# Neighbourhood attention: row maxima of single heads in two score banks, and a ring of five banks for the turned products

## The reference, cut to what matters

```python
x = x + _L0_conv_ref(_gn(x), ...)      # 12 heads over all 1024 tokens
x = x + _L1_conv_ref(_gn(x), ...)      # the layer of the change
x = x + _L2_conv_ref(_gn(x), ...)
x = x + _L3_conv_ref(_gn(x), ...)

# _L1_conv_ref
k_cat = jnp.concatenate([k, reg_k], axis=-2)
v_cat = jnp.concatenate([v, reg_v], axis=-2)
mask = make_neighbourhood_mask(KERNEL, KERNEL, h, w)          # 7 x 7, clipped at the edges
scores = jnp.einsum('bnqe,bnke->bnqk', q, k_cat) * scale
scores = jnp.where(mask_cat[None, None], scores, NEG_INF)
attn = jax.nn.softmax(scores, axis=-1)
o = jnp.einsum('bnqk,bnke->bnqe', attn, v_cat)
o = o.transpose(0, 2, 1, 3).reshape(n, h, w, nh * e)
return o @ out_w.T + out_b
```

## Time and profile before

| | us |
|---|---|
| median of three timed runs | 8417.23 |
| the three runs | 8416.32, 8417.23, 8431.45 |
| the profiled execution | 8455.42 |
| its span | 8453.7 |
| the stretch of `attend_win` in it | 2713 to about 3487 |

### The profile page before, as it was taken

How to read it: one execution, slowest core, us unless ns; L and a number is a source line. 1 busy time by engine, 2 the same in 40 slices (tenths; PEclk the granted TensorE clock), 3 DMA queues, 4 the chain that set the end, 5 groups by cost and what they waited for, 6 DMA issues and landing times. The chain is left out here.

```text
span 8453.7 us, 163553 instructions
## 1 busy us (share of the span) xinstructions
PE 7140.6 (84%) x56704; PEld 4354.6 (52%) x56704; DVE 4964.6 (59%) x7151; ACT 3849.1 (46%) x7081; POOL 2019.5 (24%) x2406
## 2 busy tenths in 40 slices
PE   3999999999866999479989999997686799999998
PEld 2555555555444656245555555553332455555555
DVE  3655555555444666545555555553878566666665
ACT  1444444444511555324444444443011577777776
POOL 3344334344210000043443443431111000000000
PEclk7999999999977898769899999998666899999999
DMA  7666766766457655567667667663122545455453
GB/s 176 127 131 115 132 131 123 138 118 123 76 166 188 123 115 112 128 132 137 123 123 130 125 121 138 120 126 78 74 77 68 128 118 129 114 124 124 114 129 83
DMA packets 502140, 1026.32 MB, mean 121 GB/s; under 512 B 80616, under 2 KB 276905, under 8 KB 460793
## 3 DMA queue, kind: packets, MB, share of 16 engines
q1 hardware_dynamic: 454198, 932.07, 50.4%
q0 software_dynamic: 47360, 86.53, 6.3%
HBM read 658.36 MB, written 358.93 MB: 120 GB/s over the span
## 5 line engine op out<-in xcount | busy, mean ns | idle before, releaser
L1616 DVE TENSOR_REDUCE a_nmp<-a_S 128x2 f32<-128x1024 f32 x1536 | 1878.4, 1224 | 1294.9 <-PE a_S L1461 1279.0
L1717 ACT ACTIVATE a_PROB<-a_T 128x512 f32<-128x512 f32 x3072 | 1667.8, 595 | 1918.7 <-PE a_T L1440 1778.4
L1310 POOL CAST a_RF<-a_RL 32x512 fp32r<-32x512 f32 x1536 | 1294.9, 843 | 1097.2 <-DVE a_RL L1644 1005.1
L2486 DVE CUSTOM_DVE_ANT_0 a_X<-a_S,a_mask 128x1024 f32<-128x1024 f32 x768 | 909.9, 1222 | 569.7 <-PE a_S L2382 566.2
L1436 PE MATMUL a_T<-a_QW,a_KW 64*128 64x512 f32 x3072 | 810.0, 519 | 283.5 <-ACT a_PROB L1717 206.4
L2527 ACT ACTIVATE a_PROB<-a_T 128x512 f32<-128x512 f32 x1536 | 836.2, 602 | 386.0 <-PE a_T L2396 386.0
L1436 PEld LDWEIGHTS a_T<-a_QW,a_KW 64*128 64x128 f32 x3072 | 313.4, 192 | 1292.2 <-issue 1289.2
L1474 PE MATMUL a_O<-a_PROB,a_V 128*32 128x512 f32 x6144 | 916.9, 672 | 2.5 <-ACT a_PROB L1717 2.5
L2396 PE MATMUL a_T<-a_ident,a_X 128*128 128x128 f32 x6144 | 824.3, 277 | 102.3 <-DVE a_OSB L2503 98.3
L2396 PEld LDWEIGHTS a_T<-a_ident,a_X 128*128 128x128 f32 x6144 | 670.9, 141 | 303.8 <-issue 285.5
L1461 PEld LDWEIGHTS a_S<-a_KV,a_QV 64*128 64x128 f32 x6144 | 660.1, 202 | 123.9
(11 more groups left out here) (179 smaller groups left out, 9120.8 us busy)
## 6 DMA issues: line engine op xcount, KB each, us to landing
a_QV<-a_part_rows SPq DMA_DIRECT2D x384, 256.0 KB, 7.6
a_rel_rows<-a_RF SPq DMA_DIRECT2D x96, 1024.0 KB, 9.3
a_K<-part_rows SPq DMA_DIRECT2D x576, 128.0 KB, 3.8
a_part_rows<-a_part SPq DMA_DIRECT2D x48, 1024.0 KB, 10.9
a_QV<-a_part_rows SPq DMA_DIRECT2D x384, 128.0 KB, 8.1
a_QV<-a_rel_rows SPq DMA_DIRECT2D x384, 128.0 KB, 7.0
a_QW<-a_rel_rows SPq DMA_DIRECT2D x192, 256.0 KB, 9.3
a_mask<-L_mask SPq DMA_DIRECT2D x48, 1024.0 KB, 10.5
```

Of the source, the lines that this page charges most:

```text
L1310: nc.gpsimd.tensor_copy(dst, src).then_inc(permuted, 1)
L1616: nc.vector.tensor_reduce(nmp[:, qh, c, 2 * pr:2 * pr + 2, kh], S[:, pr], AX.X, ALU.max).then_inc(s_done, 1)
L1717: nc.scalar.activation(PROB[:, s % PRING, 2 * pr + sd], T[:, slot(("st", s, pr, sd))], ACT.Exp).then_inc(t_act, 1)
L2486: nc.vector.tensor_tensor_reduce(out=X[:, v % 2, c, g], in0=S[:, sd].rearrange("p a b -> p (a b)"), in1=mask[:, n % 2, g, c], scale=1.0, s ...
```

## The change

The straight products go from pairs to single heads. A turn has MAXIMA = 2 * G = 8 of them, each one matmul of 256 or 284 columns into one bank, and S has two banks instead of four; single n waits for the reduction of single n - 2. DVE reduces each head by itself (one maximum, 128 x 226 or 128 x 284). ITEMS gives singles 0 to 3 to kc = 0, 4 and 5 to kc = 1, 6 and 7 to kc = 2, which are the same heads at the same steps. The two banks go to the ring: RING = 5, so a tile in T waits for the tile five places back in SEQ. The order of SEQ, the tails and all other work stay. From L786 on, line numbers are smaller by one in the changed kernel.

```diff
-    RING, PRING, BUFS = 3, 3, 3
+    RING, PRING, BUFS = 5, 3, 3
...
-    ITEMS = {0: (0, 1), 1: (2,), 2: (3,)}
+    MAXIMA = 2 * G
+    ITEMS = {0: (0, 1, 2, 3), 1: (4, 5), 2: (6, 7)}
...
-        S = ctx.enter_context(nc.psum_tensor(f"{name}_S", [P, 2, 2, BANK], F32))
+        S = ctx.enter_context(nc.psum_tensor(f"{name}_S", [P, 2, BANK], F32))
...
             def straight(t, i):
                 u, quad = divmod(t, QUADS)
-                tile, pr = divmod(i, 2)
-                n, s = 4 * t + i, u % BUFS
+                tile, g = divmod(i, G)
+                n, s = MAXIMA * t + i, u % BUFS
...
                 need(pe, s_done, n - 1)
                 alone(pe)
                 at, width, _, _ = SPANS[(quad // 2, tile)]
-                for sd in range(2):
-                    g = 2 * pr + sd
-                    last = nc.tensor.matmul(S[:, n % 2, sd, 0:width],
-                                            Q_[0:ROWS, s, g, WIDE * quad + P * tile:WIDE * quad + P * tile + P],
-                                            K[0:ROWS, s, g, NEAR * quad + at:NEAR * quad + at + width], start=True, stop=True)
-                last.then_inc(s_ready, 1)
+                nc.tensor.matmul(S[:, n % 2, 0:width],
+                                 Q_[0:ROWS, s, g, WIDE * quad + P * tile:WIDE * quad + P * tile + P],
+                                 K[0:ROWS, s, g, NEAR * quad + at:NEAR * quad + at + width], start=True, stop=True
+                                 ).then_inc(s_ready, 1)
...
             def row_max(t, i):
-                tile, pr = divmod(i, 2)
-                n = 4 * t + i
+                tile, g = divmod(i, G)
+                n = MAXIMA * t + i
                 _, _, at, width = SPANS[(t % QUADS // 2, tile)]
                 eng.wait_ge(s_ready, n + 1)
-                nc.vector.tensor_reduce(nm[:, t % 2, tile, 2 * pr:2 * pr + 2], S[:, n % 2, :, at:at + width], AX.X, ALU.max,
+                nc.vector.tensor_reduce(nm[:, t % 2, tile, g:g + 1], S[:, n % 2, at:at + width], AX.X, ALU.max,
                                         negate=True).then_inc(s_done, 1)
 
             def combine(t):
                 e = t % 2
-                eng.wait_ge(s_done, 4 * t + 4)
+                eng.wait_ge(s_done, MAXIMA * (t + 1))
```

More of the change, by code:

```diff
@@ L854, in _ @@
             pe.wait_ge(wide_set, 1)
-            for i in range(4):
+            for i in range(MAXIMA):
                 straight(0, i)
             turn_max(0)
-            for i in range(4):
+            for i in range(MAXIMA):
                 straight(1, i)
```

## The result

| | before | after |
|---|---|---|
| median of five timed runs, us | 8417.2 | 8512.2 |
| range of the five | 8397.8 to 8449.5 | 8494.0 to 8521.7 |
| ratio | | 1.0089 (95% interval 1.0071 to 1.0108) |
| the profiled execution | 8455.4 | 8494.0 |
| the stage in it (first score product to the end of the last projection) | 772.5 | 830.5 |

The change makes the kernel slower by 75 us (60 to 91), which is the ratio's 0.89% of 8417. The two medians themselves are 95 us apart; in the later experiments the kernel before had medians of 8433.6 (19 runs), 8434.7 (24) and 8436.1 (13), so the 8417.2 of the table is some 18 us low. The forecast was 8467, with 8432 to 8525 as its range. The stage, which is all that the change touches, is 58 us longer in the two profiled executions.

What follows compares the result with a forecast made beforehand. The prediction took the stage to be bound by a chain through three engines, none of them full. Four quad terms gave 2.07 us a unit, x 24 units = +50 us on 8417, so 8467 us, range 8432 to 8525.

Steps and rivals of the forecast that it cites:

- the mechanism: Step 0: third and fourth singles wait for the first two reductions; V comes 1.04 or 1.18 us after r0.
- projection, then 226: Quad with a projection, then 226 columns: V at 3031.26 for 3031.00, +0.26 us.
- projection, then 284: Quad with a projection, then 284 columns: 0.14 us more after r0, 0.05 more before, +0.35 us.
- sums: Quad behind the sums: r0 moves 0.63 us earlier; +0.18 or +0.56 us by unit, middle +0.37 taken.
- reciprocals: Quad behind the turned reciprocals: DVE multiplies outputs first, r0 at 3023.44, V at 3024.48 for 3023.39, +1.09 us.
- unit: One unit of the neighbourhood stage: its four quads add 2.07 us, 32.5 us for 30.4.
- rival 2: TensorE's pauses keep the clock low through the reciprocals' quad: some 1.5 us a unit, 8503; chance 15%, 3% for worse.
- The ring: Five banks remove the tail tiles' wait for the casts: 2 x 0.58 + 0.63 + 0.39 = 2.18 us a unit.
- L785's waits: Score matmuls wait for reductions some 0.4 us each, near 100 us for 2.1; forecast wrong if under 40.
- waits of the tails: The tail tiles' 50.2 us of waiting for casts nearly gone, part again at the reciprocals' turned scores.
- Reductions as said: DVE's single-head reductions in the stage: 768 of them, 0.39 to 0.45 us each.
- The step from a unit to the stage: 2.07 us a unit x 24 units = +50 us, the first unit taken at the same amount.

Runs made afterwards that it cites:

- Ring of three: Changed kernel with the ring back at three banks, two PSUM banks idle: ratio to the kernel before 1.0173.
- three banks: Changed kernel with single heads in three score banks and a ring of four: ratio to the kernel before 1.0036.
- the four at step 1: Changed kernel with four singles at step 1 and two at step 0: ratio to the kernel before 1.0028.
- packed pairs: Changed kernel, both tiles of one head packed in one bank, TensorE waiting per pair: ratio to before 0.9957; with a ring of three instead of five, 1.0005.
- one sum matmul: One 32-column matmul for the sums' eight, most normalisation left out: kernel before 8333.1 us, changed kernel 8471.4, packed pairs 8323.1.
- fillers: Two overwritten 512-column matmuls added ahead of the sums and each turned tile: changed kernel 1.0159, packed pairs 1.0031, against the kernel before.

## Why the prediction came out as it did

**The sign and the mechanism were right, one term was far too small.** The four singles of step 0 wait for the reductions of the first two, V queues behind them, and ACT and the next quad behind V. Ring of three, three banks, the four at step 1 and the packed pairs each move the time the way this says: the less V depends on a reduction, the less is lost, and with no dependence the kernel is faster than before.

**The terms, each against the traces.** From V to V, in us, over the 21 steady units of before and of after; a quad is named by the tail tile that stands in front of its last V's scores:

| quad | forecast | before, mean | after, mean | difference | difference of the medians |
|---|---|---|---|---|---|
| projection, then 226 | +0.26 | 7.87 | 7.89 | +0.02 | +0.26 |
| projection, then 284 | +0.35 | 7.60 | 7.95 | +0.35 | +0.34 |
| sums | +0.37 | 7.67 | 8.14 | +0.47 | +0.79 |
| reciprocals | +1.09 | 8.01 | 10.06 | +2.05 | +2.49 |
| unit | +2.07 | 31.2 | 34.0 | +2.9 | |

Means and medians differ because the low stretch isn't alike in all units of before: in 13 of the 21 it takes 3.0 to 3.6 us, in the others 7 to 13.5. The quads taken one by one:

- Projection, then 226 columns: forecast +0.26. The quad from 3076.99 to 3084.86 is 7.87 us for 7.61 in the earlier trace rows: +0.26, exactly. The exactness is luck, for both halves were a little off and cancel: r0 comes 1.24 us after the casts' end, not 1.32, and V 1.12 us after r0, not 1.04.
- Projection, then 284: forecast +0.35. V at r0 + 1.25 (3057.15, 3058.40) for the 1.18 forecast; the quad as a whole came as forecast.
- Sums: forecast +0.37, the middle of +0.18 and +0.56. In most units of before V stands close to r0 behind the sums, as in the second unit of the earlier trace rows, so +0.56 was the one to take; and V is r0 + 1.46 for the 1.18 counted, since the clock is falling there (3065.07, 3066.53), which makes 0.84 for the 0.79 of the medians:

```profile
3065.07 0.81 DVE L888 TENSOR_REDUCE a_nm<-a_S 128x1 f32<-128x284 f32 x2
...
3065.66 0.94 PE L785 MATMUL a_S<-a_K,a_Q 79*128 79x284 f32 x2 [0.79 <-DVE a_nm L888]
...
3066.53 1.08 PE L814 MATMUL a_O<-a_PROB,a_V 128*32 128x256 f32 x8
```

- Reciprocals: forecast +1.09, measured +2.05 in the mean: **this is the mis-sized term**, and the unit's excess over the forecast (2.9 for 2.07) is about as large. In the unit of the timelines the quad took 10.46 us for 7.36. From the end of the casts to V it is 3.65 us (3073.34 to 3076.99) for 1.66 in the earlier trace rows (3021.73 to 3023.39), +1.99 where the forecast counted +1.09; the other 1.1 us lie ahead of the casts. In the unit ahead of it, where the clock is back as the casts begin (at 3038), the same stretch is 2.84 us (3039.78 to 3042.62), +1.18: there the forecast's own term holds, and the quad is 9.64 us. The windows say why. After:

```profile
3065.00:3067.00 2.00, 1.33 (x10) 0.78 (x10) 1.60 (x5) 0.58 (x2) 0.00 (x0) 0.57 1.19 144
3067.00:3069.00 2.00, 2.00 (x15) 1.46 (x8) 0.40 (x2) 0.37 (x1) 0.00 (x0) 0.50 0.90 198
...
3073.00:3075.00 2.00, 2.00 (x14) 1.21 (x7) 1.50 (x7) 0.20 (x1) 0.00 (x0) 0.50 0.23 63
3075.00:3077.00 2.00, 1.54 (x9) 1.13 (x9) 1.52 (x4) 1.09 (x2) 0.00 (x0) 0.87 0.00 0
```

Before, at the same place:

```profile
3014.00:3016.00 2.00, 2.00 (x13) 1.76 (x13) 1.38 (x3) 0.99 (x2) 0.00 (x0) 0.74 1.12 169
3016.00:3018.00 2.00, 2.00 (x14) 1.16 (x14) 1.07 (x2) 0.47 (x2) 0.00 (x0) 0.50 0.97 128
3018.00:3020.00 2.00, 2.00 (x19) 1.45 (x19) 1.32 (x2) 1.09 (x2) 0.00 (x0) 0.91 1.04 223
```

The clock is back after some 3.4 us before and after some 10 us in the changed kernel, and in between every block of matmuls is run at the lower level. Of the 21 units of after, 14 are like this one and 7 have 6 to 7 us at the lower level. That is rival 2 as it was written, down to the quad, and I had given it 18%, as if it excluded the forecast. Both came. Its size: of the units of before one took 30.33 us with a clock of 0.94 (3.6 us low) and the next 33.79 with 0.80 (13.5 low), which is 0.35 us for each us at the lower level. A line through all 21 units has the same slope in before, but 0.19 in after. The change adds 8.9 - 5.6 = 3.3 such us, an estimated 0.6 to 1.2 us of the 2.9 that a unit gained; the rest, 1.7 to 2.3, is the handshake less the ring, for 2.07 in the forecast. The two units:

```profile
3073.30:3103.63 30.33, 27.35 (x216) 17.86 (x217) 21.21 (x49) 16.23 (x32) 0.79 (x1) 0.94 0.61 119
3103.63:3137.42 33.79, 31.74 (x216) 20.61 (x217) 21.40 (x49) 16.23 (x32) 0.79 (x1) 0.80 0.55 109
```

The second of them also shows that the prediction read too much into one unit: it said that in each unit the clock is back before the turned maximum of the next quad. Here it wasn't, nor in two more of the 21, and their quads of the reciprocals and of the 226 columns took 9.57 and 9.3 us, for the 7.6 to 7.8 of most others. The 30.4 us of a unit that it started from is such a common unit as well; the mean is 31.2.

The evidence against rival 2 was the last unit, where the clock stayed at 1.00 with PE busy for 11.86 of 14.00 us. It said that a share of pauses is harmless; it did not say so of one long pause right where the clock is falling.

**The ring.** Forecast 2.18 us a unit. Measured 1.4 in packed pairs, 1.4 with the clock at its upper level, 3.2 with singles. With the clock's share taken out by the same 0.35 it is 1.4 + 0.35 x 2.1 = 2.2 in packed pairs and 3.2 - 0.35 x 3.8 = 1.9 with singles (2.5 by 0.19), which are estimates. The cleanest comparison is the two kernels with one sum matmul, at a clock of 1.00, and there the median quads tell the terms: the two projections gain 0.63 and 0.67 us (7.60 to 6.97, 7.57 to 6.90) for 0.58 forecast each; the sums gain 0.18 (5.78 to 5.60; the edit makes their tile shorter in both kernels) for 0.63; the reciprocals lose 0.12 (6.48 to 6.60) where +0.39 was forecast. TensorE's 14.6 us of waiting for the casts in front of the turned reciprocals are gone there, but 9.6 us of idle time stand in their place for which the profile names no releaser. So the projections' terms hold, and why the ring gives nothing to the quad of the reciprocals stays open.

**The expected signs.** L785's waits: 58 us, not near 100, but above the 40 that was set as the bound. The row counts one wait a turn, the third matmul's. The fourth's is inside the merged line: the two take 0.66 us at 3084.28 and 0.46 at 3083.39, where nothing waits, and the trace shows these 0.2 us as busy time. The waits of the tails are gone. Reductions as said. The unit is 34.0 us, not 32.5. This row stands in place of 50.2 us of waits for the casts, so it doesn't give the cost by itself; the 54.8 us of ACT's copies do better.

**The sum.** 50 us were forecast, 58 stand in the stage and 75 (60 to 91) in the timed runs. The step from a unit to the stage, 24 equal units with the first one paying like the rest, was wrong too: the steady units alone add 60 us, the start and the end of the stage nothing (-2). Of the 45 us between the forecast 8467 and the median 8512, some 18 are the base of 8417, which later runs of before put at 8434 to 8436, and 8 are the stage. The range held the result because it took in the price of the clock. What I can't account for is the rest, the difference between 58 and 75: one pair of traces can't say how much of it lies in the stage.

Left open: what this handshake would cost with the clock held up (nothing that I tried held it in this kernel), and why the fillers made its low stretch longer.

## What to carry to other kernels

Before splitting a pair of banks into singles, count how many are issued in a row: with two banks the third waits for the reduction of the first, and what is queued behind it on TensorE waits along. Free banks by packing what is really read (here 226 + 284 of 512 columns, with the second matmul writing over the first one's surplus) and keep the handshake at its old grain; the reading engine could then go finer at no cost that was measurable here (1.0005). If a handshake must be, put it where the reading engine is idle. And a new pause on TensorE can be paid twice, once as a wait and once in the clock: look at the granted clock around it in the trace, in several units and not in one, and add the clock's price to the wait's, not as a rival to it.

## What the runs showed of the hardware

- A pause of 1.47 us of TensorE (after with one sum matmul), in which the granted clock fell, was followed by more than 8 us at 0.50 with PE busy for all of them. The packed kernel with the same edit, in which the score matmuls wait for reductions only 2.3 us in the whole stage, stayed at 1.00 in its steady units.
- In before, the clock falls behind sixteen matmul rows of 4 columns (eight matmuls, 1.92 us), in a window in which PE is busy for 2.00 of 2.00 us. With one of 32 columns in their place it stayed at 1.00 for 578 us, and the stage was 94 us shorter (772.5 to 678.3), the shorter tile itself included.
- Two matmuls of 512 columns at three places of a unit went with a lower mean clock in after (0.87 to 0.82).
- A reciprocal takes 358 ns for 32 columns and 3357 for 512, some 6.2 ns an element, where a maximum takes 1.04 (387 ns for 226 and 448 for 284 in after).
- In the packed kernel four single reductions back to back (1020 elements) take 1.41 us; two pairs took 1.16 for 904 elements, which is 1.28 for 1020. So each instruction more costs some 0.06 us.
